# Two graph layers and a masked 12-head attention: the probabilities transposed by DMA in two fp16 halves

## The reference

```
layer:   u = h h^T / sqrt(D);  a = softmax(u) * adj;  attn = a / (sum(a) + 1e-10)
         ctx = triu(attn) (h Wl^T) + diag(attn) (h Ws^T) + tril(attn) (h Wr^T)    # with biases
         h = relu(layernorm(ctx) * g + b)
y      = layernorm(x + h2)
heads:   q, k, v = y Wq + bq, y Wk + bk, y Wv + bv            # 12 heads of 32
         scores = q k^T / sqrt(32) + beta * adj, and -9e15 where adj <= 0
         out = softmax(scores) v
result = layernorm(y + out)
```

## Time and profile before

| | |
|---|---|
| median of 2 runs | 1994.72 us (1994.0 to 1995.43) |
| the profiled execution's own time | 1997.11 us |
| its span | 1995.4 us |
| busy: PE, DVE, ACT, POOL | 1871.1, 1625.2, 1262.6, 754.4 us |
| mean granted TensorE clock | 0.97 |
| DMA moved | 147.18 MB |

### The profile page before, as it was taken

How to read it: one execution, slowest core, us unless ns; L and a number is a source line. 1 busy time by engine, 2 the same in 40 slices (tenths; PEclk the granted TensorE clock), 3 DMA queues, 4 the chain that set the end, 5 groups by cost and what they waited for, 6 DMA issues and landing times.

```text
span 1995.4 us, 43610 instructions
## 1 busy us (share of the span) xinstructions
PE 1871.1 (94%) x14656; PEld 1806.1 (91%) x14656; DVE 1625.2 (81%) x5318; ACT 1262.6 (63%) x3612; POOL 754.4 (38%) x778
## 2 busy tenths in 40 slices
PE   4789999999999999999999999999999999999965
PEld 4779999999999999999999999999999999999954
DVE  3458888888888888888888888888888888888864
ACT  2346666666676666667666666766666676666644
POOL 1123343434334343433434343344434434443430
PEclk8789999999999999999999999999999999999975
DMA  3122223333222333322233332223233222333220
GB/s 110 56 72 67 66 63 83 85 84 83 67 65 63 84 84 85 83 67 68 59 85 82 84 86 66 61 65 88 80 83 88 64 61 67 88 81 83 81 48 16
DMA packets 144548, 147.18 MB, mean 74 GB/s; under 512 B 17596, under 2 KB 144328, under 8 KB 144328
## 3 DMA queue, kind: packets, MB, share of 16 engines
q1 hardware_dynamic: 133424, 131.20, 24.7%
q10 hardware_dynamic: 10904, 13.20, 1.8%
HBM read 56.25 MB, written 12.58 MB: 34 GB/s over the span
## 4 chain that ended last, share of the span: by engine, by line
PE 79%; DVE 15%; issue 2%; ACT 2%; SPq 0%; ACTq 0%; POOL 0%; DMA 0%; POOLq 0%; DVEq 0%
PE bank_w L349 41%; PE bank_m L349 10%; PE bank_u L349 7%; PE bank_p L490 7%; PE bank_o L349 5%; PE bank_s L349 4%; DVE pT_lo L843 2%; DVE normed L795 2%; DVE masked L837 2%; DVE normed L781 2%; DVE stats_y L798 2%; PE bank_t L366 1%; PE bank_u L429 1%; PE bank_t L356 1%; PE bank_t L377 1%
## 5 line engine op out<-in xcount | busy, mean ns | idle before, releaser
L635 ACT ACTIVATE prob<-masked,hmin 128x256 f32<-128x256 f32 x768 | 383.8, 503 | 73.5 <-DVE hmin L837 66.5
L837 DVE CUSTOM_DVE_ANT_0 masked<-bank_s,bias_adj 128x256 f32<-128x256 f32 x768 | 292.5, 419 | 71.9 <-PE bank_s L349 67.4
L642 ACT ACTIVATE pT_hi<-bank_p 128x512 f16<-128x512 f32 x384 | 227.8, 593 | 97.4 <-PE bank_p L490 79.0
L843 DVE TENSOR_TENSOR pT_lo<-bank_p,pT_hi 128x512 f16<-128x512 f32 x384 | 262.6, 684 | 13.8 <-ACT pT_hi L642 11.9
L490 PE MATMUL bank_p<-ident,prob 128*128 128x128 f32 x1536 | 242.8, 282 | 23.3 <-DVE pT_lo L843 22.7
L584 ACT ACTIVATE hlrh<-bank_w 128x384 fp32r<-128x384 f32 x256 | 120.7, 483 | 174.8 <-PE bank_w L349 174.8
L935 POOL TENSOR_SCALAR v_rest<-adj_in 128x512 f32<-128x512 f32 x32 | 61.8, 1930 | 412.1 <-issue 397.2
L349 PE MATMUL bank_w<-w_graph0h,hT_ach 128*128 128x384 f32 x576 | 203.7, 354 | 12.3 <-DVEq L699 12.3
L490 PEld LDWEIGHTS bank_p<-ident,prob 128*128 128x128 f32 x1536 | 178.2, 144 | 36.4 <-issue 29.6
L349 PE MATMUL bank_w<-w_graph1h,hT_bh 128*128 128x384 f32 x576 | 201.6, 350 | 5.3 <-DVEq L699 5.3
L742 DVE TENSOR_TENSOR hlrl<-bank_w,hlrh 128x384 fp32r<-128x384 f32 x256 | 141.5, 553 | 69.2 <-ACT hlrh L584 69.2
(11 more groups left out here) (200 smaller groups left out, 5879.7 us busy)
## 6 DMA issues: line engine op xcount, KB each, us to landing
x_in<-in_x SPq DMA_DIRECT2D x64, 384.0 KB, 3.2
adj_in<-in_adj SPq DMA_DIRECT2D x96, 256.0 KB, 3.3
q_st<-qk_hi SPq DMA_DIRECT2D x256, 96.0 KB, 2.2
k_st<-qk_hi SPq DMA_DIRECT2D x256, 96.0 KB, 2.3
q_st<-qk_lo SPq DMA_DIRECT2D x128, 96.0 KB, 2.2
k_st<-qk_lo SPq DMA_DIRECT2D x128, 96.0 KB, 2.2
out<-result ACTq DMA_DIRECT2D x32, 384.0 KB, 2.5
prob<-in_L_gnn_Wl SPq DMA_DIRECT2D x2, 192.0 KB, 3.8
```

Source lines behind the costliest of these rows:

```text
L635: nc.scalar.activation(prob[:, h % 2, i, :], masked[:, i, :], ACT.Exp, bias=hmin[:, i, h:h + 1], scale=-1.0, accum_out=hsum[:, i, h:h + 1] ...
L642: nc.scalar.activation(pT_hi[:, h % 2, :, :].rearrange("p j i -> p (j i)"), bank_p[:, :], ACT.Copy).then_inc(s_pt_hi, 1)
L837: ve.tensor_tensor_reduce(masked[:, i, :], bank_s[:, i * S:(i + 1) * S], bias_adj[:, i, :], -SCALE, BIG, ALU.add, ALU.min, hmin[:, i, h:h ...
L843: ve.tensor_tensor(pT_lo[:, h % 2, :, :].rearrange("p j i -> p (j i)"), bank_p[:, :], pT_hi[:, h % 2, :, :].rearrange("p j i -> p (j i)"), ...
```

## The change

The probabilities of a head are no longer transposed by TensorE. VectorE's masking writes into prob, the exponential runs in place and keeps no sum. In the new step weights ScalarE copies prob to fp16 (halves, index 0) and VectorE subtracts that from prob into halves, index 1, all in SBUF. SP then issues one DMA that transposes both halves, a source of 128 partitions by 1,024 fp16, into pT, eight blocks of 128x128. attend reads them from there. Each part of the values gets a 33rd column, one in the first part and zero in the others, so the row sum of the probabilities comes out of attend's own product, and VectorE inverts it for two heads at a time ahead of L853's reduction. bank_p becomes a second score bank. SP gets a list of its own in ORDER. The copies of queries and keys go by quarters of the heads (every fourth head is in one quarter), each with its semaphore, and the heads are worked in the order HEADS. To make room, the layers' bias rows lie in one row tile, and small columns share one tile.

```
+VC = 33
+HEADS = (0, 4, 8, 9, 1, 5, 2, 6, 10, 11, 3, 7)
 ORDER "pe":   all weights.* left out, the other steps in the same order
 ORDER "act":
-        turn_y.0-1 scores.8-1 weights.7-1 turn_y.1-1 scores.9-1 turn_y.2-1 weights.8-1 scores.10-1 q.0
-        weights.9-1 q.1 h_norm.0 q.2 scores.11-1 k.0 weights.10-1 turn_h.0 k.1 k.2 turn_h.1 weights.11-1
+        turn_y.0-1 scores.8-1 weights.8-1 turn_y.1-1 scores.9-1 weights.9-1 turn_y.2-1 scores.10-1
+        weights.10-1 q.0 q.1 h_norm.0 q.2 scores.11-1 weights.11-1 k.0 turn_h.0 k.1 k.2 turn_h.1 turn_h.2 v.0
 ...
+        scores.0 weights.0 c_store.0 scores.1 weights.1 b_proj.4 b_proj.5 scores.2 weights.2 scores.3
+        weights.3 scores.4 weights.4 a_scores.0 b_norm.0 a_proj.0 a_turn.0 b_apply.0 a_proj.1 scores.5
+        weights.5 scores.6 weights.6 a_proj.2 a_proj.3 a_proj.4 b_norm2.0 scores.7 weights.7 a_proj.5""",
 ORDER "dve":
+        scores.8-1 weights.7-1 turn_y.0-1 a_proj.5-1 attend.5-1 scores.9-1 weights.8-1 turn_y.1-1 a_mix.0-1
+        scores.10-1 weights.9-1 turn_y.2-1 attend.7-1 a_mix.1-1 h_norm.0 q.0 scores.11-1 weights.10-1 q.1 q.2
+        h_apply.0 k.0 attend.9-1 weights.11-1 turn_h.0 k.1 k.2 turn_h.1 turn_h.2 attend.11-1 v.0 v.1
 ...
+    "sp": """
+        weights.6-1 weights.7-1 weights.8-1 weights.9-1 weights.10-1 weights.11-1 c_adj.0 a_x.0 q_stack.0
+        q_stack.1 q_stack.2 q_stack.3 b_adj.0 k_stack.0 k_stack.1 k_stack.2 k_stack.3 b_x.0 a_adj.0 weights.0
+        weights.1 weights.2 weights.3 weights.4 weights.5""",
 ...
-        bank_s = bank("bank_s")
-        bank_p = bank("bank_p")
+        bank_s = [bank("bank_s0"), bank("bank_s1")]
 # SP: a quarter of the copies is 3 DMAs; the waits of c_adj, a_x, b_adj, b_x, a_adj are those of before
+            def weights(t, k):
+                s = t - 2
+                sp.wait_ge(s_pt_lo, NH * s + k + 1)
+                wait(sp, s_pv, NH * s + k - 1)
+                sp.dma_start_transpose(pT[:, k % 2, :, :], halves[:, k % 2, :, :, :].rearrange("p i a s -> p (i a s)")
+                                       ).then_inc(s_pt[k % 2], 16)
 # PE, attend
-                pe.wait_ge(s_pt_lo, NH * s + h + 1)
+                pe.wait_ge(s_pt[b], 16 * (NH // 2 * s + k // 2 + 1))
 ...
-                        mm(bank_o[:, at:at + VP * HD], pT_hi[:, h % 2, j, i * P:(i + 1) * P], vp, j == 0, False)
-                        last = mm(bank_o[:, at:at + 2 * HD], pT_lo[:, h % 2, j, i * P:(i + 1) * P], vp[:, 0:2 * HD],
+                        mm(bank_o[:, at:at + VP * VC], pT[:, b, 4 * i + j, :], vp, j == 0, False)
+                        last = mm(bank_o[:, at:at + 2 * VC], pT[:, b, 4 * i + 2 + j, :], vp[:, 0:2 * VC],
 # ACT, scores and weights
-                    nc.scalar.activation(prob[:, h % 2, i, :], masked[:, i, :], ACT.Exp, bias=hmin[:, i, h:h + 1],
-                                         scale=-1.0, accum_out=hsum[:, i, h:h + 1]).then_inc(s_prob, 1)
+                    nc.scalar.activation(prob[:, k % 2, i, :], prob[:, k % 2, i, :], ACT.Exp, bias=hmin[:, i, k:k + 1],
+                                         scale=-1.0).then_inc(s_prob, 1)
+                act.wait_ge(s_prob, NT * (NH * s + k + 1))
+                wait(act, s_pt[k % 2], 16 * (NH // 2 * s + k // 2))
+                nc.scalar.activation(halves[:, k % 2, :, 0, :], prob[:, k % 2, :, :], ACT.Copy).then_inc(s_pt_hi, 1)
 # DVE, scores, weights and attend
+                wait(dve, s_pt_lo, NH * s + k - 1)
+                    ve.tensor_tensor_reduce(prob[:, k % 2, i, :], bank_s[k % 2][:, i * S:(i + 1) * S], bias_adj[:, i, :],
+                                            -SCALE, BIG, ALU.add, ALU.min, hmin[:, i, k:k + 1]).then_inc(s_msk, 1)
+                ve.tensor_tensor(halves[:, k % 2, :, 1, :], prob[:, k % 2, :, :], halves[:, k % 2, :, 0, :], ALU.subtract
+                                 ).then_inc(s_pt_lo, 1)
+                ve.reciprocal(hinv[:, :, a:b + 1:b - a], parts[:, :, :, HD, 0])
+                ve.tensor_reduce(att[:, :, a:b + 1:b - a, :], parts[:, :, :, 0:HD, :], AX.X, ALU.add).then_inc(s_att, 1)
```

More of the change, by code:

```diff
@@ L50 @@
[L50 to L59 removed]
+        turn_y.0-1 attend.5-1 turn_y.1-1 scores.9-1 a_mix.0-1 attend.6-1 scores.10-1 attend.7-1 turn_y.2-1
@@ L64 @@
+        h_apply.0 k.0 attend.9-1 weights.11-1 turn_h.0 k.1 k.2 turn_h.1 turn_h.2 attend.11-1 v.0 v.1
         b_scores.0 c_stat.0 b_proj.0 turn_x.0 b_proj.1 c_stat.1 turn_x.1 b_mask.0 c_norm.0 scores.0 c_apply.0
-        b_turn.0 scores.1 turn_x.2 scores.2 b_proj.4 weights.0 b_proj.5 a_scores.0 scores.3 weights.1 b_mix.0
-        attend.1 scores.4 weights.2 b_mix.1 b_norm.0 a_mask.0 b_apply.0 a_proj.0 weights.3 a_turn.0 scores.5
-        a_proj.1 attend.3 scores.6 weights.4 b_resid.0 b_resid.1 weights.5 b_norm2.0 scores.7 a_proj.4 b_out.0
@@ L71 @@
 }
 STAGE_D = ("c_sum", "c_stat", "c_norm", "c_apply", "c_store")
-STAGE_C = ("q", "k", "v", "scores", "weights", "attend")
+STAGE_C = ("q", "k", "v", "scores", "weights", "attend", "c_adj", "q_stack", "k_stack")
 def schedule(engine, t, batches):
@@ L268, in pipeline @@
                 todo = schedule(order, t, NB)
-                for n, step in enumerate(firsts):
+                for n, step in enumerate(firsts if order != "sp" else ()):
                     if step in todo:
@@ new lines, in stack, with c_adj, a_x @@
+                    sp.dma_start((q_st, k_st)[side][slot * HD:(slot + 1) * HD, r::HPG, :].bitcast(F32),
+                                 part[r * HD:(r + 1) * HD, side, :, :].bitcast(F32)).then_inc(s_stack["qk"[side]][r], 16)
+            def c_adj(t, _k):
+                wait(sp, s_em, 2 * (layer_a(t - 1) + 1) if t <= NB
+                     else 2 * (layer_b(t - 1) + 1))
+                sp.dma_start(adj_in[:, :, :], adj_v[t - 2]).then_inc(s_adj["c"], 16)
+            def a_x(t, _k):
+                wait(sp, s_resid, (t - 1) * NT)
+                if t == 1:
+                    sp.wait_ge(s_tx_pe, NC)
+                sp.dma_start(x_in[:, :, :], x_v[t]).then_inc(s_xa, 16)
@@ new lines, in b_adj, with b_x @@
+            def b_adj(t, _k):
+                if t >= 2:
+                    wait(sp, s_badj, t - 1)
+                else:
+                    wait(sp, s_em, 2 * (layer_a(t - 1) + 1))
+                sp.dma_start(adj_in[:, :, :], adj_v[t - 1]).then_inc(s_adj["b"], 16)
+            def b_x(t, _k):
+                if t < NB:
+                    wait(sp, s_tx_pe, NC * (t + 1))
+                else:
+                    wait(sp, s_resid, (t - 1) * NT)
+                sp.dma_start(x_in[:, :, :], x_v[t - 1]).then_inc(s_xb, 16)
@@ new lines, in a_adj @@
+            def a_adj(t, _k):
+                if t >= 1:
+                    wait(sp, s_em, 2 * (layer_b(t) + 1))
+                sp.dma_start(adj_in[:, :, :], adj_v[t]).then_inc(s_adj["a"], 16)
+            def weights(t, k):
[4 more added lines that the diff above has]
+                                       ).then_inc(s_pt[k % 2], 16)
@@ L334, in load, with body_and_weights @@
                                  ).then_inc(s_stage[n], 16)
-            def body_and_weights(t):
-                body(t)
+            steps = {
+                "c_adj": c_adj, "a_x": a_x, "b_adj": b_adj, "b_x": b_x, "a_adj": a_adj, "weights": weights,
+                "q_stack": lambda t, r: stack(t, 0, r), "k_stack": lambda t, r: stack(t, 1, r),
+            }
+            def body_and_weights(t, todo):
+                run(steps, todo)
                 for n in {0: (0, 1), 1: (2,)}.get(t, ()):
                     load(n)
-            for t in range(NB + 2):
-                body_and_weights(t)
+            pipeline(sp, "sp", body_and_weights)
             sp.wait_ge(s_out, 16 * NB)
```

240 lines of the change are left out of this document (96 added, 144 removed).

## The result

| | before | after |
|---|---|---|
| median of 2 runs | 1994.72 us | 2204.59 us (2202.63 to 2206.54) |
| ratio, 95% interval | | 1.105 [1.1023, 1.1077] |
| profiled execution, its span | 1997.11, 1995.4 | 2206.54, 2204.8 |
| busy PE, DVE, ACT, POOL (us) | 1871.1, 1625.2, 1262.6, 754.4 | 1814.2, 1664.5, 1211.7, 811.3 |
| mean granted TensorE clock | 0.97 | 0.94 |

A forecast was written before the change was run, and what follows sets the result against it. A once-per-batch loop through SP's late heads' adjacency load, GpSimd and VectorE was taken as the bound: 51.9 + 10.8 = 62.7 us against 58.4, over 31 periods plus about 4 us, giving 2132 us; range 1980 to 2400.

The forecast's parts named there:

- The loop: Once per batch weights.11's transpose, c_adj, q.0, v.0 and VectorE's list back to weights.11 set the period: 62.7 us.
- Second leg: From weights.11 to v.0: SP's transpose, waiting behind its data, adjacency landing, q.0 and hops; 10.8 us, bounds 8.4 and 18.
- First leg: VectorE from v.0 to weights.11: 48.8 us of work plus 3.1 idle, 51.9 us, bounds 48.0 and 55.
- the port: VectorE's subtraction, both operands in SBUF, slows beside GpSimd through the shared port: 0.8 us per batch, 2.1 at most.
- the ends: Outside the 31 periods, about 4 us added for the last head, whose transpose lies open at the end.
- TensorE's relief: TensorE loses 12 heads' transposes but gains wider V: 5.3 us less per batch, 1833 us if nothing else takes its place.
- Rival 1: The loop is short, at least 56.4 us, and TensorE's relief shows; chance 0.05 under 1957 us, 0.20 for 1957 to 2037.
- Rival 2: Transposes fill SP or the DMA engines, deciding from 3.7 us each; times above 2250 us, chance 0.25.
- Rival 3: The wait behind c_adj is covered; other loads set a period of 55 to 58 us; chance contained in Rival 1's.
- Rival 4: VectorE's subtraction or ScalarE's copy is much slower from SBUF, lengthening the first leg; bounded at 65 us in all.

The follow-up runs named there:

- e7: As e5, with each DMA transpose replaced by a plain copy of the same bytes and the reciprocal by an addition (other output): 2093.50 us, ratio 1.0480.
- e2: The changed kernel with 18 matmuls that nothing reads put on TensorE ahead of b_proj.0, filling its gap: 2162.57 us, ratio 1.0825.
- e3: The changed kernel with transposes of half the size, first 128 rows only, used for both row tiles (other output): 2186.02 us, ratio 1.0952.
- e1b: The kernel of e1 (changed kernel, c_adj.0 ahead of weights.6-1 on SP) run once more for its profile: 2152.18 us.
- e5: As e1, with SP's b_adj.0 also moved ahead of a_x.0 and the query copies, right behind weights.11-1: 2143.46 us, ratio 1.0755.
- e8: As e5, with weights.0 and weights.1 moved ahead of the loads b_x and a_adj in SP's list: 2092.00 us, ratio 1.0476.
- e1: The changed kernel with c_adj.0, the heads' adjacency load, moved on SP ahead of weights.6-1: 2161.83 us, ratio 1.0813.
- e10: As e7 (plain copies, other output), with weights.0 and weights.1 ahead of b_x and a_adj: 2080.38 us, ratio 1.0419.
- e6: As e5, with attend and weights steps moved in the lists of TensorE, ScalarE and VectorE: 2170.82 us, ratio 1.0880.

## Why the prediction was right, and where it was short

**The loop.** Right: order and mechanism as forecast, SP's transpose of head 11, then c_adj, q.0, v.0, b_proj.0. GpSimd was released by the load, VectorE waited 4.3 us per batch, TensorE 3.4, and 9.9 us lie between weights.11's end and v.0.

**Second leg: 10.8 forecast, 9.9 measured.** SP's transpose was 1.23 us, not 1.5. From c_adj's issue to q.0 are 3.2 us, where 2.7 of landing and 1.0 of waiting behind the data were counted: c_adj's median landing is 3.0 us, so it waited some 0.3 to 0.5. (The upper bound given for this leg, 18, is 18.9 by its own terms; nothing else rests on it.) q.0 5.3, as in the rows. The Trainium skill (Advanced Engine Details and Errata, X-Bar Transpose (TRN2)) calls these transposes as fast as regular DMAs; here 256 KB transposed landed 3.1 us after issue and the same bytes plain 2.3 (e7), so they are near to that but slower, and SP's issue is 1.23 against 0.46.

**First leg: 51.9 forecast, 65.55 - 9.9 = 55.7 measured.** The work was sized rightly. VectorE idles 14.0 us of an average steady period by the trace's records, and 7.3 of them in the second leg (0.86, 1.77, 0.42 and 4.22 of the passage shown), so 6.7 in the first, which leaves 49.0 of work against 48.8 forecast. Its terms: the subtraction rose from a mean of 684 ns to 773, 12 x 0.09 = 1.1 us per batch where 0.8 was taken for the port; the conversion on ScalarE takes 631 ns from SBUF, 593 before, and waits for nothing new but the transposes.

```profile
L653 ACT ACTIVATE halves<-prob 128x512 f16<-128x512 f32 x384 | 242.2, 631 | 159.6 <-DMA pT<-halves 152.5
...
L853 DVE TENSOR_TENSOR halves<-prob,halves 128x512 f16<-128x512 f32 x384 | 296.7, 773 | 9.7 <-ACT halves L653 9.7
```

**The step that was short** is the idle time of the first leg, "between none and all of it I take half, 3.1": it measured 6.7. The table of periods gives the likely reason for most of it: mean 65.36 less 62.43 without a fall is 2.9 us of clock per batch, and in the three periods without a fall VectorE idled 11.3 us, not 14.0. With three such periods the size is rough; that the clock costs time at all is e2's finding. No term of the sum had the clock. The row of the steady batch before shows 1.00 throughout, and the forecast took TensorE's durations from it while it put a new gap of over 2 us per batch into TensorE's time. With 2.9 x 31 = 91 us more the forecast would have been 2223, over the 2205 measured; the difference is at the ends, where 4 us were added and (2204.8 - 1995.4) - 31 x (65.55 - 58.4) = -12 us measured.

**TensorE's relief** was forecast as 5.3 us per batch, by starts. Its busy time per steady period was 57.2 us before; in the changed kernel it is 53.8 without a fall of the clock, 3.4 less, and 55.6 and 56.5 with 3.4 and 6.8 us at half clock, so the clock takes most of the relief back. In the time the relief is worth nothing here: VectorE and the waits hold the period.

**Rival 1** (a short loop) failed on the idle time. **Rival 2** (transposes fill SP or the DMA engines) failed: 1.23 us of SP, far below the 3.7 from which it decides, and e3 gave back 19 us. The Trainium skill (VectorE: DVE Perf Modes, The three transpose paths) has 1309 ns per 128x128 block; eight blocks landed in 3.1 us here, so they do not go one after another at that price. A mild form of this rival shows once c_adj is early: in e1b and e5 the first two heads' transposes landed in 4.1 to 4.7 us behind copies and loads. In the changed kernel itself their median was 3.1, so the forecast's sentence on this ("a landing of 4 us or more costs TensorE a wait there, which its slack covers") was not put to the test there. In e5 the cover did not hold: moving these two heads ahead of the loads (e8) was worth 51 us. That the two buffers hand the wait on to the next heads is argued, not shown. **Rival 3** (the wait behind c_adj is covered) failed: it stood open as 3.4 us of TensorE per batch. **Rival 4** was of the size forecast.

**What undoing the named cause taught.** The forecast would have expected e1 to give back nearly all. It gave 43 us, because three paths were close together (periods without a fall of the clock): the loop through c_adj (62.4 us), the first heads behind the copies and loads (62.2 in e5), and whatever sets 60.9 in e8, which no run names.

**Where the 210 us are.** SP's order: 113 together with the clock that it cost, in the steps 43 (c_adj), 18 (b_adj, a step no larger than its uncertainty) and 51 (heads 0 and 1). Left in e8: 97 us over the kernel before. Some 12 to 14 of these go with transposing as such (e8 against e10). VectorE's work per period is 52.2 us there (61.53 less 9.33 idle, from its records) against 50.1 before (58.30 less 8.17), 2.1 x 31 = 65 us if VectorE is the bound, which is argued and not shown; the rest would be the longer way of a head through DMA with two buffers. Not tried: a third buffer, and all four lists planned anew for the DMA's latency; e6, by hand, made it worse. No run undoes the rest of the change either (the new order of heads, the copies by quarters, the 33rd column, the moved steps of ScalarE and VectorE), so a part of the 97 us may be theirs. What holds e8 at 4.8% over the kernel before stays open.

## What to carry to other kernels

- When a step moves to an in-order queue, write down what now stands behind it and who waits for that. Here the step cost 1.2 us of issue, and the load behind it, once per batch, closed a loop over four engines; moving one load that way cost 284 us in a kernel without the step.
- A gap put into a busy TensorE can be paid twice. Where a sum has a new idle stretch on TensorE, work out a second case with the matmuls behind it at the half-clock rows (in the changed kernel 1.8 to 1.9 us for each 3.4 us at 1.2 GHz, by the medians of the table; the few periods of the other kernels scatter more).
- Undoing a rightly named cause returns only the distance to the next path. Look for the next path in the same list before sizing the undo: the landing of the first transfer behind a burst is not the median one.

## What the runs showed of the hardware

- A DMA transpose of 128 x 1,024 fp16 from SBUF to SBUF: 1.23 us of SP's queue, landing 3.0 to 3.1 us after issue when nothing stands ahead, 4.1 to 4.7 (medians in e1b and e5; 5.5 in the case shown) behind a burst of copies and loads. Half of it: 1.19 and 2.4 us. A plain copy of the same bytes: 0.46 and 2.3 us.
- Queue 1 counted 538928 - 133424 = 405,504 more packets for 384 transposes, 1,056 each. Its share rose from 24.7% to 49.0% without becoming the bound.
- TensorE's granted clock fell to 0.50 for 3.4 or 6.8 us at a time. At the 3.3 us of idle time before b_proj.0 it fell in 23 of 27 steady batches; in the other four the gap was as long (3.26 to 3.30 us). It fell after shorter ones too: at none of e10's 19 falls had TensorE just stood idle for more than 1.4 us at a stretch.
- A VectorE subtraction of 128 x 512 with both operands in SBUF took 0.68 to 0.69 us in the 249 of 384 cases in which no GpSimd instruction overlapped it, and beside GpSimd a median of 0.77 and up to 1.59 us (changed kernel). With one operand in PSUM (kernel before) it took 0.67 to 0.69 us in all cases, 184 of them beside GpSimd.
